# One ring of 18 tiles filled in shrinking pieces, and a matmul program that is passed through twice

## What is computed

```
entities = einsum('be,le->bl', x, W)          # 1024 x 128
s        = sum(x, axis=1)
scale    = where(s != 0, 1 / s, 1)
y        = entities * scale[:, None]
```

## Time and profile before

| what | value |
|---|---|
| time, median of 3 runs | 151.28 us (150.81 to 151.89) |
| time of the profiled execution | 151.15 us |
| its span | 149.4 us |
| mean granted TensorE clock | 0.996 |
| TensorE busy | 135.2 us (91% of the span) |
| VectorE busy | 94.5 us (63%) |
| ScalarE busy | 84.1 us (56%) |
| share of the 16 DMA engines that the main queue took | 92.6% |

### The profile page before, as it was taken

One profiled execution on the slowest core, in us unless ns is written; L12 is line 12 of the kernel. 1 busy time (PEld: TensorE's weight loads), 2 busy tenths in 40 slices (PEclk: granted clock), 3 DMA queues, 4 the chain that ended last, 5 costly groups with the idle time before them and its releaser, 6 DMA issues.

```text
span 149.4 us, 2230 instructions
## 1 busy us (share of the span) xinstructions
PE 135.2 (91%) x785; PEld 76.4 (51%) x785; DVE 94.5 (63%) x110; ACT 84.1 (56%) x129; POOL 0.7 (0%) x13
## 2 busy tenths in 40 slices
PE   0597998799999999999999999999999999999960
PEld 0244654455555555555555655655555555665530
DVE  0471953746756845955954954864864778965593
ACT  3571852735735834844843854763763677955173
POOL 1000000000000000000000000000000000000000
PEclk9999999999999999999999999999999999999998
DMA  5999999999999999999999999999999999999022
GB/s 147 404 427 459 405 454 399 449 420 425 444 410 449 410 444 420 434 434 410 454 415 434 420 439 429 410 459 410 434 425 439 408 425 416 414 406 342 16 70 75
DMA packets 5719, 58.19 MB, mean 390 GB/s; under 512 B 638, under 2 KB 1534, under 8 KB 2514
## 3 DMA queue, kind: packets, MB, share of 16 engines
q1 hardware_dynamic: 5714, 58.13, 92.6%
HBM read 57.60 MB, written 0.52 MB: 389 GB/s over the span
## 4 chain that ended last, share of the span: by engine, by line
DMA 56%; PE 35%; DVE 4%; SPq 1%; issue 1%
DMA xw<-main 56%; PE acc L417 35%; DVE y_sum L366 2%; DVE low_max L320 1%; SPq L167 1%; DVE row_sum L363 0%; SPq L163 0%; SPq L165 0%; DVE row_sum L357 0%; DVE row_sum L360 0%; DVE any_low L396 0%; PE acc L470 0%; DVE inexact L398 0%
## 5 line engine op out<-in xcount | busy, mean ns | idle before, releaser
L417 PE MATMUL acc<-parts_main,xw 128*128 128x385 bf16 x640 | 108.2, 327 | 3.8 <-DMA xw<-main 3.0
L417 PEld LDWEIGHTS acc<-parts_main,xw 128*128 128x128 bf16 x640 | 61.3, 98 | 50.7 <-issue 8.4
L320 DVE TENSOR_REDUCE low_max<-xw 128x2048 uint16 x20 | 45.5, 2278 | 0.0
L243 ACT ACTIVATE parts_main<-xw 128x512 bf16<-128x512 bf16 x20 | 12.7, 635 | 47.0 <-DMA xw<-main 37.7
L309 DVE TENSOR_TENSOR w_rest<-xw 128x512 f32<-128x512 f32 x20 | 13.8, 692 | 40.0 <-DMA xw<-main 40.0
L250 ACT ACTIVATE act_out<-xw 128x2048 bf16<-128x2048 uint16 x20 | 37.9, 1893 | 0.0
L316 DVE TENSOR_TENSOR parts_main<-w_rest 128x512 bf16<-128x512 f32 x21 | 14.6, 695 | 0.7
L246 ACT ACTIVATE parts_main<-w_rest 128x512 bf16<-128x512 bf16 x21 | 13.3, 635 | 2.0
L417 PE MATMUL acc<-parts_short,xw_short 84*128 84x385 bf16 x8 | 2.7, 522 | 5.5 <-ACT parts_short L246 5.5
L320 DVE TENSOR_REDUCE low_max<-xw_taper 128x1 f32<-128x1024 uint16 (+1 forms) x6 | 6.1, 1038 | 1.4 <-DMA xw_taper<-ends 1.3
L250 ACT ACTIVATE act_out<-xw_taper 128x1024 bf16<-128x1024 uint16 (+1 forms) x6 | 5.4, 906 | 1.7 <-DMA xw_taper<-ends 1.6
(11 more groups left out here) (50 smaller groups left out, 38.2 us busy)
## 6 DMA issues: line engine op xcount, KB each, us to landing
xw<-main SPq DMA_DIRECT2D x20, 2304.0 KB, 16.3
xw_taper<-ends SPq DMA_DIRECT2D x2, 1024.0 KB, 24.9
x_final<-ends SPq DMA_DIRECT2D x3, 512.0 KB, 27.8
xw_taper<-ends SPq DMA_DIRECT2D x1, 1408.0 KB, 21.8
xw_ramp<-ends SPq DMA_DIRECT2D x1, 1280.0 KB, 7.5
xw_taper<-ends SPq DMA_DIRECT2D x1, 1280.0 KB, 18.8
xw_taper<-ends SPq DMA_DIRECT2D x2, 512.0 KB, 27.1
xw_ramp<-ends SPq DMA_DIRECT2D x1, 704.0 KB, 4.9
```

The source lines that it names most:

```text
L243: nc.scalar.activation(parts[0:rows, 0:n, 0:L], top(words, n), ACT.Copy)
L320: nc.vector.tensor_reduce(low_max[0:rows, bass.ds(col, 1)], low(words, n), AX.XY, ALU.max).then_inc(dve_checked, 1)
L417: return nc.tensor.matmul(acc[:, b, 0:N], x, parts, start=first, stop=last)
```

## The change

- The ring is now `xw` of 18 tiles (each 1024 of x and 128 of W together), and W of every tile comes with the x of the tile three before it. The first 3 tiles of W (`w_first`) and the last 4 (`w_alone`) come by themselves.
- The 90 tiles in the ring come in 34 pieces of 1 to 4 tiles: they grow from 1 to 4 at the start and shrink to 1 at the end (`PIECES`). Each has a semaphore; GpSimd waits for them in order and adds the number of tiles to one semaphore `landed`, for which the others wait.
- TensorE waits for each tile, no more for each piece. VectorE and ScalarE work in units of 3 tiles (30 units in place of 20 main pieces and the edges): in a loop of 5 turns with 6 units each.
- A piece is issued when the unit of the ring that its last tile overwrites has been used by TensorE, VectorE and ScalarE. SyncE's program for the ring is written out, no more a loop. No taper buffers: the taper's pieces lie in the ring too.
- One x tile comes alone (`x_after`), and the last part cut by banks has 6 tiles in place of 4.
- At the end VectorE checks a quarter of each `x_final` piece and ScalarE three quarters; VectorE adds the parts of two banks in one instruction; VectorE, no more ScalarE, does the last multiplication by 1/s.
- TensorE's program of products stands in a loop of two turns, in two `If`s that are taken in the second turn only. In the first turn TensorE branches past both bodies.
- The skipped slow path is written out longer for SyncE and TensorE.

```diff
-T = 4
-SLOTS = 4
-MAIN = 20
-RAMP_X = (1, 2)
-TAPER_X = (2, 2, 2, 2, 1, 1)
-TAPER_W = (T, 6, 0, 0, 0, 0)
-LAST = 4
-FINAL = ((0, 2, 0, 4), (2, 4, 0, 4), (4, 6, 0, 4), (6, 7, 0, 4), (7, 8, 0, 2), (7, 8, 2, 4))
+UNIT = 3
+SLOTS = 6
+RING = SLOTS * UNIT
+ROUNDS = 5
+UNITS = ROUNDS * SLOTS
+LOOP = UNITS * UNIT
+PIECES = (1, 2, 3, 4, 4, 4,
+          4, 4, 4, 3, 3,
+          4, 4, 4, 3, 3,
+          3, 3, 3, 3, 2, 2, 2,
+          2, 2, 2, 2, 2, 2, 2, 1, 1, 1, 1)
+WEIGHTS_AFTER = len(PIECES) - 4
+LAST = 6
+FINAL = ((0, 2, 0, 6), (2, 4, 0, 6), (4, 6, 0, 6), (6, 7, 0, 6), (7, 8, 0, 4), (7, 8, 4, 6))
...
+        def unit_split(u):
+            return u + 2
+        ALONE_SPLIT = unit_split(UNITS + 1)
+        def used(u):
+            return u + 7
+        def dve_share(k):
+            return x_final[k].shape[1] // 4
...
+            for k, n in enumerate(PIECES):
+                pool.wait_ge(piece_in[k], 16)
+                pool.sem_inc(landed, n)
...
+            sp.dma_start(xw_short[0:short, :], edge(0)).then_inc(short_in, 16)
+            sp.dma_start(w_first[:, :], edge(1)).then_inc(first_in, 16)
+            for k, n in enumerate(PIECES):
+                if k == WEIGHTS_AFTER:
+                    sp.dma_start(w_alone[:, :], edge(2)).then_inc(alone_in, 16)
+                last_unit = (FIRST_TILE[k] + n - 1) // UNIT
+                if last_unit >= SLOTS:
+                    sp.wait_ge(products_done, used(last_unit - SLOTS))
+                    sp.wait_ge(dve_checked, used(last_unit - SLOTS))
+                    sp.wait_ge(act_checked, used(last_unit - SLOTS))
+                j = FIRST_TILE[k] % RING
+                sp.dma_start(xw[:, j:j + n, :], piece(k)).then_inc(piece_in[k], 16)
+            sp.dma_start(x_after[:, :], edge(3)).then_inc(after_in, 16)
...
+            with dve.Fori(0, ROUNDS) as i:
+                for s in range(SLOTS):
+                    u = SLOTS * i + s
+                    dve.wait_ge(landed, UNIT * u + UNIT)
+                    dve.wait_ge(top_parts_done, unit_split(u - 1))
+                    rest(unit_w(s), UNIT, (s + 1) % 2)
+                    dve.wait_ge(products_done, used(u + 1 - SLOTS))
+                    lo(parts[:, (s + 1) % SLOTS, :, :], UNIT, (s + 1) % 2, unit_split(u + 1))
+                    low_largest(unit_x(s, 0, B // 2), u + 1).then_inc(dve_checked, 1)
...
+            check(0)
+            check(1)
+            finish(0)
+            check(2)
+            finish(1)
+            check(3)
+            check(4)
+            finish(2)
+            check(5)
+            finish(3)
+            finish(4)
+            dve.wait_ge(inverse_done, len(PAIRS))
+            dve.wait_ge(y_summed, len(PAIRS))
+            nc.vector.tensor_scalar(y[:, BANKS - 1, :], y_sum[:, BANKS - 1, :], row_sum[:, BANKS - 1, 2:3], None,
+                                    ALU.mult).then_inc(y_last_ready, 1)
...
+            with pe.Fori(0, 2) as turn:
+                with pe.If(turn != 0):
+                    pe.wait_ge(ones_set, 1)
+                    pe.wait_ge(short_in, 16)
+                    wait_split(1)
+                    multiply(top(tiles(xw_short[0:short, 0:B], 1))[:, 0, :], parts_short[0:short, 0, :],
+                             first=True).then_inc(products_done, 6)
+                    with pe.Fori(0, ROUNDS) as i:
+                        for s in range(SLOTS):
+                            wait_split(unit_split(SLOTS * i + s))
+                            for j in range(UNIT):
+                                pe.wait_ge(landed, RING * i + UNIT * s + j + 1)
+                                mm = multiply(top(unit_x(s))[:, j, :], parts[:, s, j, :])
+                            mm.then_inc(products_done, 1)
+                    wait_split(ALONE_SPLIT)
+                    pe.wait_ge(after_in, 16)
+                    multiply(top(tiles(x_after[:, :], 1))[:, 0, :], parts[:, 0, 0, :])
+
+                with pe.If(turn != 0):
+                    for k in range(NF):
+                        pe.wait_ge(final_in[k], 16)
+                        for b, mm in last_tiles(k, last_parts, last_product):
+                            if b == FINAL[k][1] - 1:
+                                mm.then_inc(bank_full, 1)
```

More of the change, by code:

```diff
@@ L42, in pieces, with rec_kernel, edge, piece @@
         at += rows * cols
-    return table, at
-def rec_kernel(nc, main, ends, out, E):
+    return table
+def rec_kernel(nc, loop, ends, out, E):
     B, L = out.shape
     BANKS = B // P
+    ROW = B + L
     short = E - (TILES + LAST) * P
-    table, _ = pieces(short, B, L)
+    table = edges(short, B, L)
     ONES = PARTS * L
     N = ONES + 1
[L53 to L59, removed]
+    NF = len(FINAL)
+    CHECKS = 2 + UNITS + NF
+    FIRST_TILE = [sum(PIECES[:k]) for k in range(len(PIECES))]
+    assert 0 < short <= P and N < 512 and sum(PIECES) == LOOP and SLOTS % 2 == 0
+    assert all(a % RING + n <= RING for a, n in zip(FIRST_TILE, PIECES))
+    def edge(k):
         at, rows, cols = table[k]
         return ends[at:at + rows * cols].rearrange("(p f) -> p f", p=rows)
+    def piece(k):
+        at = FIRST_TILE[k] * P * ROW
+        return loop[at:at + PIECES[k] * P * ROW].rearrange("(p j f) -> p j f", p=P, j=PIECES[k])
     with ExitStack() as ctx:
@@ L254, in _, with low_sum @@
+                nc.scalar.activation(parts[0:rows, :, L:2 * L], rest, ACT.Copy).then_inc(top_parts_done, 1)
+            def low_sum(words, col, buf, rows=P):
+                n, f = words.shape[1:]
+                return nc.scalar.activation(tiles(act_out[0:rows, buf, 0:n * f], n), low(words), ACT.Copy,
+                                            accum_out=low_max[0:rows, bass.ds(CHECKS + col, 1)])
             act.wait_ge(short_in, 16)
-            split(xw_short[0:short, B:B + L], parts_short, 1, 0, 1, rows=short)
@@ L256, in _ @@
[L256 to L257 removed]
+            split(tiles(xw_short[0:short, B:ROW], 1), parts_short, 1, 1, 1, rows=short)
+            act.wait_ge(first_in, 16)
+            split(tiles(w_first[:, :], UNIT), parts[:, 0, :, :], UNIT, 0, unit_split(0))
             act.wait_ge(ones_set, 1)
[L259 to L260 removed]
@@ L304, in _ @@
-            scale(BANKS - 1, pair)
+            low_sum(tiles(xw_short[0:short, B // 2:B], 1), 0, 0, rows=short).then_inc(act_checked, 6)
+            with act.Fori(0, ROUNDS) as i:
+                for s in range(SLOTS):
+                    u = SLOTS * i + s
+                    act.wait_ge(landed, UNIT * u + UNIT)
+                    act.wait_ge(products_done, used(u + 1 - SLOTS))
+                    split(unit_w(s), parts[:, (s + 1) % SLOTS, :, :], UNIT, (s + 1) % 2, unit_split(u + 1))
+                    act.wait_ge(act_checked, used(u - 2))
+                    low_sum(unit_x(s, B // 2), u + 1, (s + 1) % 2).then_inc(act_checked, 1)
```

438 lines of the change are left out of this document (161 added, 277 removed).

## The result

The changed kernel takes 152.47 us (median of 5 executions, 151.61 to 152.65) against 151.23 for the kernel before: ratio 1.0074, 95% interval [1.0053, 1.0095]. It is 0.7% slower; the prediction of 147.5, with a range to 149.3, was wrong. Its profiled execution took 151.61, with a span of 149.8 and a mean granted clock of 1.0; the other four took 152.29 to 152.65 at clocks of 0.985 to 0.996.

What follows compares the result with a forecast made beforehand. The stream was taken to bound the kernel, then three end delays (4.8, 2.85, 2.15 us). Last product 144.37 - 1.9 - 0.5 = 142.0, y 143.5, span 145.6, execution 147.4, median 147.5; own range 147.1 to 147.9, wider 146.6 to 149.3.

Steps and rivals of the forecast that it cites:

- VectorE and ScalarE in the loop: Split and check of a 3-tile unit take 2.9 us of 4.12; the split comes 0 to 0.2 late in a few pieces.
- Does TensorE arrive there in time?: TensorE's work after the last 4-tile piece, landing at 72.3, ends at about 142.5, so the bound stays 142.5 us.
- Rival 4: Split of W makes TensorE late into each of 30 units; over 0.19 us each costs, 152.9 at 0.37; chance 0.06.
- 0.8 of delay left: Start of the stream: program fetches moved there still delay a DMA engine by 0.8 us, where 1.34 was lost before.
- First turn of TensorE's program: Skipping both bodies touches program pages early, so the fetch near 24 us should be gone: gain 0.5 us.
- rival 2: Program fetched again in the stream or at the last branch: 148.0, or 149.1 with one more fetch; chance 0.23.
- Matmul spacing: TensorE's matmuls follow each other at 0.164 us, 1.31 a tile, waits already met costing nothing.
- The bound of `x_final`: First `x_final` piece lands at 134.4; six tiles of products after it end at 142.5, before the gain of 0.5.
- The piece sizes: Pieces at the end of the ring shrink as fast as TensorE's 5% lead over the stream allows; bound stays 142.5.
- the relay by GpSimd: GpSimd passing landings on to TensorE: between nothing and 0.3 us a landing, moving only 142.3 to 142.5.
- the tail: End of the kernel: y 1.5 us after the last product, where it was 2.85; gain 1.35, the last 2.15 stay.
- the ring that never runs empty: SyncE's waits leave 12 or more tiles in flight, 16 us of stream; no empty queue, costed at nothing.

Runs made afterwards that it cites:

- e2: The changed kernel with `w_alone` loaded behind `w_first` and split before the loop, `x_after` waiting only for its own parts: 149.07 us, ratio 0.988 to the kernel before.
- e13: The changed kernel with only the first ring piece issued ahead of `w_first`, `w_alone` staying late: ratio 1.0041 to the kernel before, median 152.2 us.
- e1: The changed kernel without TensorE's two-turn loop and its two Ifs: ratio 1.0013 to the kernel before from four of twelve executions; median of all 12 is 152.7 us.
- e11: The changed kernel with 18 useless matmuls, in a loop of 6 turns of 3, before the wait for `w_alone`'s split: 150.95 us, ratio 1.0 to the kernel before.
- e10: The changed kernel with `w_alone` loaded and split early and the first ring piece issued ahead of `w_first` and `w_alone`: 148.29 us, ratio 0.9821 to the kernel before.
- e6: The changed kernel with `w_alone` loaded and split early and first ring pieces of 3, 3, 4, 4, 4 tiles: 149.33 us, ratio 0.9889 to the kernel before.
- e4: The kernel before with only TensorE's products put in the two-turn loop with two Ifs: 151.18 us, ratio 1.0017 to the kernel before.
- e7: The changed kernel with `w_alone` split early, larger first ring pieces and no two-turn loop: ratio 0.9929 to the kernel before, from six of ten executions.
- e9: The changed kernel with 24 useless matmuls written out before the wait for `w_alone`'s split: 154.28 us, ratio 1.0214 to the kernel before.
- e3: The changed kernel without the two-turn loop and with `w_alone` loaded and split early: ratio 0.9891 to the kernel before, median 149.58 us.
- e12: The changed kernel with `w_alone` split early, first ring piece ahead of the small weights, no two-turn loop: ratio 0.9852 to the kernel before, from five of twelve executions.
- e5: The changed kernel with TensorE's wait for `w_alone`'s split moved behind `x_after`'s products: 150.02 us, ratio 0.9939 to the kernel before.

## Why the prediction was wrong

**The step that failed** put a wait at nothing: the one of TensorE for the split of `w_alone`, outside the loop. It is in "The change part by part", under *VectorE and ScalarE in the loop* and *Does TensorE arrive there in time?*: "The end can't be earlier than the landing of any piece plus all work from its first tile on". The bound was checked for every piece of the ring, and the split was counted only inside the loop. The four tiles of W that come alone are not in a unit of the ring. Their split stands behind the last unit's split and check, and TensorE's wait for it stands in front of `x_after`. That wait is a line of the diff that the prediction quotes nowhere. Its price could have been worked out beforehand from the earlier trace rows: from the last unit's landing 0.56 + 0.56 + 1.7 for split and check, then about 0.7 + 0.7 for four tiles (0.69 for one such instruction in the earlier trace rows), some 4.2 against the 1.7 in which TensorE finishes the last tile (1.31 and what it is behind). That is 2.5 us of idle time. The runs showed 2.58 us, released by this split, and e2, which splits `w_alone` early, got it back.

**Rival 4** named the right resource (the split of W) in the wrong place. Inside the loop it was harmless: after the last 4-tile piece no two matmuls of the ring are over 0.33 apart, 0.16 more than their usual spacing, as the forecast said.

**The clock** was not in the prediction at all, since the wait wasn't. An execution with the dip takes 1.5 to 1.7 us more (e13 and e1); the changed kernel's median lies 0.86 above its profile, which has no dip. This turns "no change" into 0.7% slower: e11, which has the wait and no dip, is at exactly 1.0.

**Stream: a term mis-sized.** "I take 0.8 of delay left": the last engine is 2.31 behind the median engine, where 0.23 was without any fetch, so about 2.1 were left. Fetches near 3.9 and 10.3 us, in a stream that is already running, seem to add to transfers that are late on other engines: e1 has no fetch before 31 us and still an engine 1.85 late in the first ring piece. The 4-tile piece landed at 73.47, 1.67 later than the 71.8 that forecast and gain of 0.5 imply. In e10 it landed at 72.81, but in e11, with the changed kernel's own order, at 72.80. Which engine is late through what isn't settled: the lags don't add up over e1, e2, e6 and e10, and run from 0.97 to 2.43 over kernels with the same stream. That 0.8 was too little is shown for all of them but e11.

**First turn of TensorE's program.** It did what the diff says: no fetch in the middle of the stream. The gain of 0.5 wasn't there, and the cost was larger than weighed: the branch at L448 alone took 5.04 us. TensorE's later start is hidden by a wait for data, as the prediction had it for delays up to 1 us: 1.39 us of idle time were still left near 21 us. e4 is the clean test: 1.0017 [0.9999, 1.0035]. The Trainium skill's rule ("Runtime: NRT & Kernel Launch", section "Instruction fetch mechanics"), that a branch out of the fetched blocks stalls, would give such stalls; rival 2 names it for the last branch. The traces agree: for L448 here, and for the last branch of e7 and e9 (2.90 and 3.78 us); the changed kernel's last branch took 0.33. That the loop brings nothing holds for e4; without it half of the executions of e3, e7 and e12 were longer, for a reason that isn't shown.

**Matmul spacing.** `x_after` and the last six tiles take 9.23 us for 7 tiles, 1.318 a tile, not 1.312, though nothing waits there: 0.165 a matmul. The ring's last 46 tiles, 73.57 to 134.34, give 1.318 too, with split waits in it. Over 53 tiles it is 0.3 to 0.4.

**The sum again.** Landing 73.47 + relay 0.10 + 53 x 1.318 + 0.16 = 143.6: the last product without the wait (e2 has 143.71, from a start 0.16 later). The forecast of this bound was 71.8 + 0.35 + 69.4 + 0.16 = 141.7, a little below that of `x_final`, 142.0. It came out 1.67 later for the landing and 0.4 for the spacing, 0.25 earlier for relay and start. The bound of `x_final` came out later still in the changed kernel: 135.75 + 0.1 + 48 x 0.165 + 0.16 = 143.9. In e2, where the first `x_final` piece landed at 135.23, it is 143.4, and there the 4-tile piece binds. So in the changed kernel's own stream the wait cost 146.3 - 143.9 = 2.4 at the end, and the late stream, with a little from the spacing, the other 1.9 against the forecast of 142.0.

**What was right.** The piece sizes (TensorE unbroken from the last 4-tile piece to the end of the ring, where before it was 4.8 behind the data); the last 4-tile piece and the first `x_final` piece as the two bounds of the stream, 0.3 apart again; the relay by GpSimd (landing 62.48, products 62.58); the tail (1.37 for 1.5); the ring that never runs empty. With the wait gone these bring 1.2% (e2), and 1.8% in the best version (e10).

## What to carry to other kernels

Go through every wait of the changed engine program to the end, those outside the loops too, and for each ask what the releasing engine has queued in front of that work; the wait that costs is often not the one for the data but for a small preparation behind a big check. A gap in TensorE's work is paid twice if the clock falls after it, so read a median that lies above the profile with the mean clock of each execution before trusting the profile. A program that is touched early is not free: it moves fetches into another part of the stream, so test it alone. And before putting half a microsecond between two profiles down to an edit, look at how far kernels with the same stream lie apart.

## What the hardware showed unexpectedly

- After 2.58 us of TensorE idle time the granted clock fell to half for 3.4 us in most executions: by the mean clocks 7 of 12 in e1, 8 of 12 in e13, 3 of 5 in the changed kernel; the profiles of e1 and e13 show it. After 1.68 (e5) and 1.56 us (e11) the mean clock was 0.997 or more in all 20 executions.
- A branch of TensorE beside which the trace has a program packet of 16384 bytes took 4.4 to 5.2 us at the start of the stream (ten kernels) and 2.9 and 3.8 just after it (e7, e9); the same last branch without one takes 0.33 to 0.46. 24 more matmuls in the program were enough to make the one into the other (e9).
- A delay of one DMA engine of 1.25 us stayed to the last transfers of a full stream: the lag is 1.46 at 27 us and 1.49 at 129 us in the kernel before.
- The same transfers in the same order, on one queue, had their last engine 0.97 to 2.43 us behind the median one, in four kernels that differ only in TensorE's program (the changed kernel, e5, e9 and e11).
